# The opening reordered: squares of W1 and W3 in ScalarE's gaps, scales in two parts, two tiles of forms under chunk 1, W2's second transform in steps 1 to 3

## What is computed

```python
kv_latent = ln(x) @ W_to_kv.T;  c = kv_latent @ W_compress.T;  ch = layernorm(c) * gamma + beta
q, k, v = ch @ W_q_comp.T, ch @ W_kv_comp.T (split)
q, k = rope(q), rope(k)
o = softmax(causal(q @ k.T / 8)) @ v
x = x + (o @ W_comp2lat.T) @ W_to_kv + (...) @ W_out_res.T + b_out_res
hidden = fwht(silu(ln(x) @ W1.T) * (ln(x) @ W3.T))          # width 2048
x = x + hidden @ W2.T
```

## Time and profile before

| | us |
|---|---|
| median of 3 runs | 2367.87 (2367.05 to 2370.82) |
| the profiled execution, its own time | 2371.3 |
| its span | 2369.5 |
| first `product` of step 0 starts | 181.05 |
| third `product` of step 0 starts | 193.82 |
| step 1 starts | 213.87 |
| step 4 starts | 268.10 |

### The profile page before, as it was taken

The page is one execution under the profiler, slowest core; times in us unless marked ns, Lnnn a source line. Parts: engine busy times, 40 slices in busy tenths (PEclk is TensorE's granted clock), DMA queues, the critical chain, the costliest instruction groups (busy, mean ns, idle before and its releaser), DMA issues. The chain is left out here.

```text
span 2369.5 us, 28477 instructions
## 1 busy us (share of the span) xinstructions
PE 2204.2 (93%) x10674; PEld 1059.8 (45%) x10674; DVE 1436.9 (61%) x2727; ACT 1051.9 (44%) x1577; POOL 229.9 (10%) x213
## 2 busy tenths in 40 slices
PE   5655889999999999999999999999999999999999
PEld 3322444444444444444444444444444444444444
DVE  6545676676656656566756666566655756563333
ACT  4643645544354354434454454544454353532221
POOL 1023644400000000000000000000000000000000
PEclk8758899999999999999999999999999999999999
DMA  6343222233222331233222331233212322223221
GB/s 262 109 164 120 99 101 83 98 125 101 97 74 77 109 119 65 89 104 112 92 72 69 130 125 65 74 116 115 92 57 80 129 98 81 80 85 111 80 80 52
DMA packets 59561, 236.50 MB, mean 100 GB/s; under 512 B 6432, under 2 KB 6560, under 8 KB 54048
## 3 DMA queue, kind: packets, MB, share of 16 engines
q1 hardware_dynamic: 59424, 234.68, 28.5%
HBM read 194.81 MB, written 39.85 MB: 99 GB/s over the span
## 5 line engine op out<-in xcount | busy, mean ns | idle before, releaser
L744 PE MATMUL PF<-XF,WS 128*128 128x512 f16 x1792 | 687.9, 384 | 23.2 <-ACT PF L1112 15.1
L745 PE MATMUL PF<-XF,WS 128*128 128x512 f16 x1792 | 686.3, 383 | 0.0
L746 PE MATMUL PF<-XF,WS 128*128 128x512 f16 x1792 | 686.2, 383 | 0.0
L768 PE MATMUL PD<-W2S,H 128*128 128x512 f16 x1024 | 389.9, 381 | 2.0 <-DVE H L1692 2.0
L769 PE MATMUL PD<-W2S,H 128*128 128x512 f16 x1024 | 389.6, 380 | 0.0
L770 PE MATMUL PD<-W2S,H 128*128 128x512 f16 x1024 | 389.1, 380 | 0.0
L1123 ACT ACTIVATE SH<-PF,afs 128x512 f32<-128x512 f32 x256 | 176.0, 687 | 368.0 <-PE PF L746 367.0
L744 PEld LDWEIGHTS PF<-XF,WS 128*128 128x128 f16 x1792 | 177.3, 99 | 233.9 <-issue 48.2
L1684 DVE SCALAR_TENSOR_TENSOR SH<-PF,afs,SH 128x512 f32<-128x512 f32 x256 | 191.6, 748 | 136.2 <-ACT SH L1123 113.4
L746 PEld LDWEIGHTS PF<-XF,WS 128*128 128x128 f16 x1792 | 176.7, 99 | 215.9 <-issue 7.7
L1131 ACT ACTIVATE H<-SH 128x1024 f16<-128x1024 f32 x128 | 135.2, 1056 | 310.5 <-DVE SH L1684 310.5
(11 more groups left out here) (306 smaller groups left out, 2380.6 us busy)
## 6 DMA issues: line engine op xcount, KB each, us to landing
WS<-wscr SPq DMA_DIRECT2D x112, 896.0 KB, 4.6
W2S<-w2scr SPq DMA_DIRECT2D x30, 1024.0 KB, 4.8
xraw<-xT SPq DMA_DIRECT2D x58, 256.0 KB, 4.4
ring<-x SPq DMA_DIRECT2D x56, 256.0 KB, 4.3
wscr<-WS SPq DMA_DIRECT2D x16, 896.0 KB, 3.6
out<-ring SPq DMA_DIRECT2D x56, 256.0 KB, 4.2
XF<-w SPq DMA_DIRECT2D x16, 512.0 KB, 4.9
RAW<-w13t SPq DMA_DIRECT2D x16, 512.0 KB, 3.3
```

Of the source, the lines that this page charges most:

```text
L744: pe.matmul(bank, wh, th, start=i < 2 and j == 0, stop=False, skip_group_check=True)
L745: pe.matmul(bank, wh, tl, start=False, stop=False, skip_group_check=True)
L746: m = pe.matmul(bank, wl, th, start=False, stop=j == 1, skip_group_check=True)
L768: pe.matmul(PD[:, t % 2, :], th, wh, start=j == 0, stop=False)
```

## The change

It reorders the lists of all five engines in the opening, and moves some of the work into the first steps. Nothing of the main loop's own work is changed.

- **Squares.** `norms(h, i)` is now one instruction for one of the two halves, writes over the rows themselves instead of into a scratch area in `WS`, and the 32 calls stand singly among the attention calls of both chunks. `square2` uses one scratch area.
- **Scales.** `scales(h0, h1, n)` is called twice: for tiles 0 to 3 after four tiles of squares, and for 4 to 15 in step 0 (f = 4).
- **Forms.** `diagonals(0)`, `(1)`, `scale_rows(0)`, `(1)` (now into the banks `G` and `U`) and `forms_high(0)`, `forms_low(0)` stand within the attention of chunk 1. `scale_rows(2)` goes to step 0 (f = 1).
- **W2's scale.** GpSimd's all-reduce is replaced by a matmul with ones (`sums`, f = 6) and a copy, and the maximum over partitions by a sum; `scale2` stands at f = 8.
- **W2's second transform.** `hadamard2(i)` and both parts of `split2(i)` stand at f = 9 + i, i = 0 to 15, one behind each product of steps 1 (from its third), 2 and 3 (to its fourth). `load_half(2)` and `(3)` are issued at f = 13 and 17 and the four `store_w2` at f = 13, 17, 21, 25. `had16` is loaded over `had` when the first transform is through.

```diff
-SCALE_AT = {7 * k + 5 + y_held(7 * k + 5): k + 3 for k in range(NH - 3)}
+SCALE_AT = {1: 2} | {7 * k + 5 + y_held(7 * k + 5): k + 3 for k in range(NH - 3)}
+SPLIT_AT = {9 + i: i for i in range(16)}
+SPLIT_END = {9 + 4 * i + 4: i for i in range(4)}
+SUMS_AT = 6
...
+            def load_had16():
+
+                w.wait_ge(p_fm, NH)
+                sp.dma_start(had, cst[:, NCST:NCST + 128]).then_inc(d_had, 16)
...
             load_raw(0)
             store_half(0)
-            store_half(1)
             norm_rows(7)
             norm_rows(8)
-            store_half(2)
             norm_rows(9)
             norm_rows(10)
+            store_half(1)
+            norm_rows(11)
+            norm_rows(12)
+            load_raw(1)
+            norm_rows(13)
+            norm_rows(14)
+            norm_rows(15)
+            store_half(2)
             store_half(3)
-            for h in range(11, 16):
-                norm_rows(h)
+            load_had16()
             load_half(0)
             load_half(1)
-            load_raw(1)
-            store_w2(0)
-            load_half(2)
-            store_w2(1)
-            load_half(3)
             store_forms(0)
             load_raw(2)
             store_forms(1)
-            store_w2(2)
-            store_w2(3)
...
+                    if s == 0 and 7 * h + j in SPLIT_END:
+                        i = SPLIT_END[7 * h + j]
+                        if i < 2:
+                            load_half(i + 2)
+                        store_w2(i)
...
+            def sums():
+
+                w.wait_ge(v_g2, 2)
+                w.wait_ge(a_xn, 3)
+                pe.matmul(G[:, 0:2], ones.broadcast_to([128, 128]), st[:, 2:4], start=True, stop=True).then_inc(p_g2, 1)
...
+                    if k == SUMS_AT // 7 and i == SUMS_AT % 7:
+                        sums()
+                    if s == 0 and f in SPLIT_AT:
+                        hadamard2(SPLIT_AT[f])
...
+            def norms(h, i):
+
                 w.wait_ge(d_n[h % 7], 16 * (h // 7 + 1))
...
+                r = rows[:, h % 7, i * 512:(i + 1) * 512]
+                ac.activation(r, r, ACT.Square, accum_out=st[:, c:c + 1]).then_inc(a_nm, 1)
...
+                if s == 0:
+                    if f == SUMS_AT - 2:
+                        scales(4, NH, 2)
+                        sums()
+                    if f == SUMS_AT + 2:
+                        scale2()
+                    if f in SPLIT_AT:
+                        split2(SPLIT_AT[f])
...
             diagonals(0)
-            w.wait_ge(v_g2, 2)
-            gp.partition_all_reduce(st[:, 4:6], st[:, 2:4], 128, bass.bass_isa.ReduceOp.max).then_inc(g_max, 1)
+            diagonals(1)
             forms(0)
-            diagonals(1)
             forms_low(0)
```

More of the change, by code:

```diff
@@ L1171, in _ @@
             high1(0, 1)
+            high1(0, 2)
             exps1(0, 3)
-            high1(0, 2)
             high1(0, 3)
-            hadamard(2)
-            hadamard(3)
-            values(1)
-            square2(1)
-            hadamard(4)
-            hadamard(5)
-            trans1(0, 0, 0)
-            rope_k(1)
+            hadamard(7)
+            hadamard(8)
+            rope_k(1)
+            trans1(0, 0, 0)
+            scale_rows(0)
+            norms(4, 1)
+            rope_q(1)
@@ L1236, in _ @@
+            norms(14, 1)
+            xtrans1(0, 2)
+            norms(15, 0)
+            xtrans1(0, 3)
+            norms(15, 1)
             tokens_high(0, 0)
+            xtrans1(1, 0)
+            xtrans1(1, 1)
             tokens_high(0, 3)
[L1238 to L1247 removed]
@@ L1248, in _ @@
-            tokens_high(0, 1)
-            for i in range(8, 16):
-                split2(i)
-            scale_rows(2)
-            for i in (2, 4, 5, 6):
-                tokens_high(0, i)
+            xtrans1(1, 2)
+            xtrans1(1, 3)
+            tokens_high(0, 1)
+            tokens_high(0, 2)
+            tokens_high(0, 4)
+            tokens_high(0, 5)
+            tokens_high(0, 6)
             forms_high(1, 0)
@@ L1833, in _ @@
             tokens_low(0, 5)
-            tokens_sum(0, 6)
             tokens_low(0, 6)
             forms_low(1)
-            sv.after(kept["scale2"])
             def fill(k, j):
```

462 lines of the change are left out of this document (241 added, 221 removed).

## The result

| | before | after |
|---|---|---|
| median, us | 2368.89 (2367.05 to 2370.82, 4 runs) | 2307.11 (2304.87 to 2308.58, 4 runs) |
| profiled execution, its own time | 2371.3 | 2304.87 |
| its span | 2369.5 | 2303.1 |
| last attention row of the opening is through | 125.5 | 105.1 |
| third `product` of step 0 starts | 193.82 | 125.30 |

The ratio after to before is 0.9738, 95% interval 0.9721 to 0.9755: the change takes 61.8 us off the medians, about a fortieth. The prediction was 2316, with a range of 2300 to 2340; it was right on the side and within the range, and 9 us too high.

What follows compares the result with a forecast made beforehand. The opening was taken to be bound by the order of the lists, each engine waiting for another, with none full. 47.3 + 17.5 - 2 - 11 = 51.8 us gain, giving 2319.5 profiled and 2316 median, range 2300 to 2340.

Steps and rivals of the forecast that it cites:

- Term 1: From the attention's end to the third product: 68.3 us falls to 21, gain 47.3.
- The walk: Hand trace of the new lists in the opening: 19.9 us from attention to third product, attention's end at 105.8.
- Term 2: Attention of chunk 1: its end comes at 108 instead of 125.5, gain 17.5 us.
- Rival (c): Attention of chunk 1: GpSimd holds up VectorE in full, 9.7 us instead of 2.2, total 2323.5; chance 0.09.
- Term 3: Step 0: the hole for transposed rows moves along unchanged, added scales and sums cost 2 us.
- The scales' 2 us: Step 0: 14 operations of scales and 3 of sums on VectorE ahead of `hidden(0, 1)` cost 2 us.
- Term 4: Steps 1 to 3 take in the whole second transform: cost 11 us, bounds 0 and 26.9.
- this wait would get longer: Steps 1 to 3: PE's 5.1 us wait for `copy_b(2)` grows, with five more low parts on VectorE.
- (b): Steps 1 to 3: the second transform sets their pace, costing the full 26.9 us, total 2332; chance 0.12.
- (d): Steps 1 to 3: second transform with no overlap, 50 us where 11 stand, 2355 alone; chance 0.03.
- its late load: Start of step 3: `load_half(3)` lands 0.5 us into the step, where `hadamard2(12)` needs it; a few us, no more.
- steps from 4 on stay as long: Main loop from step 4 on: nothing differs, each step as long as before, no gain or cost.

Runs made afterwards that it cites:

- forms_at_end: The changed kernel with the float16 parts of tile 0's forms, and tile 1's forms, moved back behind the attention; 2309.8 us, ratio 0.9751.
- before_xt_first: The kernel before, with two loads of transposed rows for chunk 2 issued ahead of the last two W2 stores; 2365.9 us, ratio 0.9983.
- w2_in_opening: The changed kernel with W2's second transform, its scale and the second part of the scales back in the opening; 2338.1 us, ratio 0.9872.
- scales_one_later: The changed kernel with transposed-row loads ahead of tile 1's forms store, and second scales, sums and `scale2` one product later; 2312.4 us, ratio 0.9757.
- run 10: Not a label: "In the second run 10 ran" counts 10 matmuls in the unaltered changed kernel's second run; 2308.0 us, ratio 0.9743.
- late_tile1_early_scales: The changed kernel with earlier transposed-row loads, token parts and tile 1's forms taken from ahead of the third product, second scales at f = 2; 2308.4 us.
- late_tile1: The changed kernel with earlier transposed-row loads, and token parts and tile 1's forms taken from ahead of the third product; 2307.2 us, ratio 0.9741.

## Why the prediction was right, and where it was off

**Bound.** The forecast rested on PE, VectorE and ScalarE each having idle time in the opening, so that order and not work was the bound. Right: the busy times of VectorE and ScalarE over the span moved by 5 us and less, the time by 62. PE's busy time fell by 20 us for as many matmuls (2204.2 to 2184.0), since more of them ran at the high level of the clock (the granted clock over the span is 0.982, and was 0.967); the forecast had no term for that.

**Term 1**, 47.3 forecast, 48.1 measured. The walk gave 19.9 us and 21 was taken; it is 20.2. The two parts that were taken off this path and were tested are the second transform (35.6) and the 24 squares (9.7 net of what they cost the attention).

**Term 2**, 17.5 forecast, 20.4 measured. The first exponential of chunk 1 was forecast at 67 and came at 66.4, the last at 91 and came at 91.2. The walk ended at 105.8 without any cost for GpSimd; 2.2 was added for it, and the attention ended at 105.1. That does not make the cost nothing. In `forms_at_end` the attention ends 4.5 us earlier, and the operations that it moves on ScalarE and VectorE are 1.77 and 0.94 us. If these cost their whole length, about 1.8 is left for GpSimd's `forms_low(0)` and tile 1's burst; if they cost less, as the squares do, it is more. The burst of tile 0 stayed where it was, and no run tells its cost. So GpSimd cost the attention 1.8 us or more, and the walk, 105.8 without any cost, was 2.5 us or more too long elsewhere; where, no run tells.

The forecast read the four-column operation of the earlier trace rows as one with its scalar and one input in SBUF. In the kernel (`norm1`) it has two inputs in SBUF and a constant as scalar, so the rule that the forecast takes from the Trainium skill, SBUF — State Buffer, "Who interferes with whom", covers it as it stands. Beside the burst of tile 0, in the kernel after, an operation that takes 0.68 us by itself (at 182.86 in the same kernel) took 1.64:

```profile
57.71 1.64 DVE L1472 TENSOR_TENSOR Kl<-H,Kh 64x512 fp32r<-64x512 f32 x1
```

```profile
57.21 3.27 POOL L1986 TENSOR_TENSOR WX<-RAW,sc 128x512 f32<-128x512 f32 x2
```

Rival (c), 9.7 us of cost and an attention that ends at 115.5, is refuted by the end at 105.1. What stays argued is the gain itself: no run undoes the new order of chunk 1's calls, with the transforms, squares and copies still in the gaps, so that it makes the 20.4 us is read from the rows, where the exponentials come when the walk had them.

**Term 3**, -2 forecast, +3.05 measured. This is the step that failed: "their issue waits for tile 1's forms, which keep their place ... so this hole moves along unchanged". The issue does keep its place, but not the queue ahead of it. I had looked at what the loads wait for to be issued, and not at the 2 MB of stores that went out 1.4 us before them. `before_xt_first` shows that by itself (4.15 us less in step 0), `w2_in_opening` brings the hole back. The scales' 2 us was right: PE's wait behind them is 2.03, and where it goes, in `scales_one_later`, the rest of step 0 is 2.3 us shorter.

**Term 4**, 11 forecast, 8.5 measured in the profile (9.5 in the second run of the same kernel). The size came near, and part of that is luck. The 16 transforms took about 16 us of PE, where 17.6 was taken: most ran at the high level of the clock, like the one at 161.71, behind which the next product starts 0.86 later, and two at the low level took 1.70 and 1.86. Half of the 13.4 us of holes, 6.7, was to come off. PE's idle time in the three steps fell by only 2.7, from 13.4 to 10.7: the wait of 5.12 us for `copy_b(2)` is 0.75 now, but others grew. What made up for it was not in the forecast. In the kernel before 28 of the 126 product matmuls of these steps ran at the low level, 12 of them behind that wait of 5.12 us; now it is 6, and none in step 2, whose granted clock rose from 0.75 to 1.00. In a row they start 0.43 us apart at the low level and 0.22 at the high one, so 22 fewer are some 4.7 us: 16 - 2.7 - 4.7 is 8.6. In the second run 10 ran at the low level, which is most of its 1 us more. PE behind the wait for `copy_b(2)` in the kernel before:

```profile
238.24 0.63 PE L745 MATMUL PF<-XF,WS 128*128 128x512 f16 x1
```

PE in the kernel after, steps 1 to 3:

```profile
161.71 1.02 PE L719 MATMUL PD<-H,cst_s 128*128 128x512 f32 x2
...
167.79 0.39 PE L767 MATMUL PF<-XF,WS 128*128 128x512 f16 x1 [0.75 <-ACT PF L1139]
168.01 0.38 PE L768 MATMUL PF<-XF,WS 128*128 128x512 f16 x1
...
197.15 1.13 PE L719 MATMUL PD<-H,cst_s 128*128 128x512 f32 x2 [0.58 <-DVE W2S L1704]
```

That this wait would get longer was said against the gain, and did not come. Rivals (b) and (d) had PE stand in the transforms for VectorE's parts: two such waits are in the trace, 0.26 and 0.58 us. VectorE is busy 47.7 us of the three steps, forecast 51. Rival (b) also misread its late load: 242.6 is 12.6 us into step 2 of the kernel before, not 12.3, and 8.6 us more end 0.9 into step 3. In the kernel after `load_half(3)` went out at 174.2, 9 us ahead of step 3, and no transform waited for it.

**The sum.** 48.1 + 20.4 + 3.05 - 8.5 = 63.1 against 51.8: of the 11.3 us between them term 3 is 5, term 2 is 3, term 4 is 2.5, term 1 is 0.8. The runs that undo a part account for 31 (second transform), 8.6 (squares) and 2.7 us (forms) of the 61.8 between the medians; the remaining 19.5 or so is about the size of term 2, which no run undoes. The forecast that steps from 4 on stay as long was right but for the granted clock, which differs from one execution of a kernel to the next.

**What stays open.** Whether 1 to 3 us can be had from the earlier loads is not settled by the times. No order tried puts the late tile 1 and the scales so that neither meets GpSimd's burst nor delays `scale2`; splitting the second scales once more was not tried, nor the scales one product later with `scale2` left at its place. The order of chunk 1's calls was not undone by itself, and the cost of tile 0's burst on GpSimd was not measured.

## What to carry to other kernels

When a step keeps its place but a transfer ahead of it in the queue goes away, read the transfer's time from issue to landing against what was issued just before it, not only against what releases the issue. Work put singly into the gaps of a chain cost that chain a sixth of its own duration for the squares (2.5 us for 24 of 0.61; between an eighth and a third, with the spread of the attention's end), but the forms, on three engines, cost about all they saved: ask of each moved piece which other engine it slows. Work that fills a wait of PE can pay twice: here the wait shrank, and the matmuls behind it ran at the high level of the clock. And a third product 4 us earlier bought nothing, since VectorE's operations ahead of the next mark then met GpSimd's burst; follow the gain up to the next mark before counting it.

## What the runs showed of the hardware

- **VectorE beside GpSimd.** Operations on 12 or 24 columns, 0.17 us each by themselves, took 0.57 to 1.26 us beside GpSimd's `tensor_tensor` on SBUF. In `late_tile1_early_scales` and `late_tile1` there are eleven of them, and each ends 0.03 to 0.04 us behind the end of a GpSimd instruction. A `tensor_tensor` of 128 x 768 took 0.94 us alone (at 84.71 in the kernel after, where GpSimd does nothing), and 2.88 when it ran beside GpSimd's of 128 x 1024, which itself took 2.82 where its mean over 16 is 2.18. GpSimd and VectorE in the kernel after:

```profile
124.03 2.82 POOL L1997 TENSOR_TENSOR WS<-WX,WS 128x1024 f16<-128x1024 f32 x1 [30.43 <-ACT WS L1117]
```

```profile
123.66 1.22 DVE L1715 TENSOR_TENSOR XF<-XS,XF 128x1024 f16<-128x1024 f32 x1
124.79 2.88 DVE L1711 TENSOR_TENSOR WS<-WX,WS 128x768 f16<-128x768 f32 x1
```

  These rows read as turns: GpSimd's instruction is recorded from 124.03, while VectorE's token part runs to 124.88, and ends 1.97 behind it; VectorE's next is recorded from 124.79, and ends 0.82 behind GpSimd's end at 126.85. The Trainium skill, SBUF — State Buffer, "Who interferes with whom", has the loser block fully, and lets `tensor_scalar` contend when it enters a two-port mode. The ends in these rows agree with that.
- **Loads behind stores.** The same two loads of 256 KB took 8.45 and 8.4 us from issue to first use with two stores of 1 MB issued 1.4 us ahead of them, and 5.4 and 4.9 us without.
- **The granted clock.** Steps 3, 7, 8 and 9 come in two lengths each in the kernels here, 1.0 to 1.7 us apart, with the granted clock of the step at 0.92 and 0.85 (step 3) or 1.00 and 0.92 (step 7), in two executions of one program; in step 9 the clock is alike (0.91 and 0.92), and the matmuls at the low level stand ahead of a wait or behind it. Of a difference of 3 us between two profiled spans of this kernel, all may be this.
